# The front of a two-layer graph kernel: statistics, adjacency turns and the first exponentials in another order

## The reference

```
deg = max(sum(adj != 0), 1)
h   = max(layernorm(x), 0)
# layer 0: gated sum of an attention and a plain convolution
attn_a = sigmoid([adj @ h, h] @ Wa.T + ba);   attn_b = sigmoid([adj @ h, h] @ Wb.T + bb)
g  = h @ W_sa;   scores = (g @ a_left)[:, None] + (g @ a_right)[None, :]
e  = where(adj != 0, exp(-leaky_relu(scores, 0.01)), 0)
x_a = (e / (sum(e) + 1e-5)) @ g
x_b = adj @ (h @ W_gcnb) + b_gcnb
x  = x + sigmoid(attn_a * x_a + attn_b * x_b)
# layer 1
h  = max(layernorm(x), 0)
x  = x + relu((dinv * (adj + I) * dinv @ h + h) @ W + b),   dinv = rsqrt(deg)
```

## Time and profile before

| | |
|---|---|
| profiled execution | 611.8 us, its span 610.0 us |
| median of 3 runs | 610.74 us (609.37 to 611.44) |
| TensorE matmuls busy | 593.4 us, 97% of the span, 5265 of them |
| VectorE, ScalarE, GpSimd busy | 425.2, 362.4, 255.5 us |
| mean granted TensorE clock | 0.993 |
| chain that ended last | TensorE 82%, VectorE 5%, DMA 4%, issue 4%, GpSimd 4%, ScalarE 2% |

### The profile page before, as it was taken

The page is one execution under the profiler, slowest core; times in us unless marked ns, Lnnn a source line. Parts: engine busy times, 40 slices in busy tenths (PEclk is TensorE's granted clock), DMA queues, the critical chain, the costliest instruction groups (busy, mean ns, idle before and its releaser), DMA issues.

```text
span 610.0 us, 13250 instructions
## 1 busy us (share of the span) xinstructions
PE 593.4 (97%) x5265; PEld 508.4 (83%) x5265; DVE 425.2 (70%) x811; ACT 362.4 (59%) x878; POOL 255.5 (42%) x361
## 2 busy tenths in 40 slices
PE   7889998999999999999999999999999999999996
PEld 5446687888888888888888888888888888888886
DVE  6897885999998999899989989988753121111111
ACT  3687667797887979797979788979642000000000
POOL 3664313554453435343525276313132374435433
PEclk8999999899999999999999999999999999999999
DMA  8908399957566565647474745010400486546401
GB/s 198 225 3 113 111 134 249 203 83 182 94 150 121 123 134 110 146 98 162 81 177 67 190 52 79 2 19 1 130 2 18 113 318 215 174 157 193 144 20 35
DMA packets 55801, 73.60 MB, mean 121 GB/s; under 512 B 20027, under 2 KB 47933, under 8 KB 54331
## 3 DMA queue, kind: packets, MB, share of 16 engines
q0 software_dynamic: 28544, 22.15, 26.5%
q1 hardware_dynamic: 24754, 46.42, 23.5%
q10 hardware_dynamic: 2441, 4.20, 2.2%
HBM read 69.31 MB, written 22.16 MB: 150 GB/s over the span
## 4 chain that ended last, share of the span: by engine, by line
PE 82%; DVE 5%; DMA 4%; issue 4%; POOL 4%; ACT 2%; ACTq 0%; POOLq 0%; DVEq 0%
PE accE L786 11%; PE accE L788 11%; PE accE L787 11%; PE accA L764 10%; PE accA L765 10%; PE accA L831 7%; PE accA L830 7%; PE accE L830 4%; PE accE L831 4%; DMA stage<-in_adj_dram 3%; POOL stage L369 1%; DVE bst L933 1%; PE pw L803 1%; PE accA L847 1%; PE pw L805 1%
## 5 line engine op out<-in xcount | busy, mean ns | idle before, releaser
L786 PE MATMUL accE<-HI,Z 128*128 128x257 f16 x676 | 185.2, 274 | 2.4 <-DVE wm L1078 2.1
L788 PE MATMUL accE<-HI,E 128*128 128x257 f16 x676 | 184.8, 273 | 0.0
L787 PE MATMUL accE<-LO,Z 128*128 128x256 f16 x676 | 184.7, 273 | 0.0
L549 ACT ACTIVATE Z<-LO,sr 128x256 f32<-128x256 f32 x338 | 151.4, 497 | 35.6 <-PE accE L788 35.6
L764 PE MATMUL accA<-HI,adjT 128*128 128x260 f16 x676 | 154.0, 273 | 0.0
L765 PE MATMUL accA<-LO,adjT 128*128 128x258 f16 x676 | 154.0, 273 | 0.0
L558 ACT ACTIVATE Z<-Z,sr 128x256 f32<-128x256 f32 x338 | 150.1, 496 | 0.2
L1034 DVE TENSOR_TENSOR Z<-adjT,Z 128x512 f32<-128x512 bf16 x169 | 127.0, 751 | 17.1 <-ACT Z L558 16.1
L1040 DVE TENSOR_TENSOR E<-Z 128x512 bf16<-128x512 f32 x169 | 129.0, 763 | 5.8
L369 POOL DMA_DIRECT2D stage<-in_adj_dram x96 | 59.3, 649 | 93.0 <-DVE adjT L1026 88.6
L831 PE MATMUL accA<-LO,adjT 128*128 128x256 f16 x416 | 91.6, 273 | 0.0
(11 more groups left out here) (127 smaller groups left out, 721.0 us busy)
## 6 DMA issues: line engine op xcount, KB each, us to landing
adjT_store<-adjT SPq DMA_DIRECT2D x11, 1664.0 KB, 6.3
stage<-in_adj_dram POOLq DMA_DIRECT2D x48, 192.0 KB, 5.0
stage<-in_adj_dram POOLq DMA_DIRECT2D x36, 224.0 KB, 5.2
adjT<-adjT_store SPq DMA_DIRECT2D x7, 896.0 KB, 6.0
adjT<-adjT_store SPq DMA_DIRECT2D x7, 768.0 KB, 6.0
stage<-adjT_store SPq DMA_DIRECT2D x4, 896.0 KB, 6.4
stage<-adjT_store SPq DMA_DIRECT2D x4, 768.0 KB, 5.8
out_dram<-late ACTq DMA_DIRECT2D x11, 256.0 KB
```

The lines of the kernel that those rows point to most:

```text
L549: ins = act.activation(Z[:, n % RING, v], slw[:, m], ACT.Relu, bias=sr99[:, t:t + 1], scale=1.0 - SLOPE)
L786: pe.matmul(dst[:, 0:D + 1], zhi, HI[:, t, 0:D + 1], start=(t == 0), stop=False)
L787: pe.matmul(dst[:, 0:D], zhi, LO[:, t, 0:D], start=False, stop=False)
L788: ins = pe.matmul(dst[:, 0:D + 1], zlo, HI[:, t, 0:D + 1], start=False, stop=(t == TILES - 1))
```

## The change

- Statistics: one row pair a step (pair s + 4 at step s) instead of two; GpSimd's and VectorE's followers take one pair each instead of batches of one to four. The prologue takes pairs 0 to 5 instead of 0 to 4.
- Adjacency of block 0 is turned in four instructions at steps 4, 5, 6, 7 instead of two and two at 5 and 6; block 1 at 11 to 14 instead of 10 and 11; block 2's first chunk at u = 2 and 4 of block 1, and its second at 7 and 9. `tr_ok` counts each instruction, so all waits on it are doubled.
- Block 0: `neighbours(0, u)` stays at step u + 6, `unit(0, u)` goes to step u + 10 (it was u + 7). `leaky` and `expo` go from u + 5 and u + 6 to u + 8 and u + 9, `mask` and `split` from u + 6 to u + 9. The steps now run to 22; four neighbours of block 1 stand among the last of them.
- TensorE: `turn(1)`, `turn(2)` and `project(0)` stand between the halves of `dense(0)` and `dense(1)`; the first steps are set out anew, with two added waits of ScalarE's `turned` for `project`.
- ScalarE: gate_exp(0), gated_b(0) and el go into block 1 at u = 3, 6 and 1, where they stood before it; gated_b(1) goes into block 2. VectorE: gate_args(0), gates(0), row_sums(0) at u = 1, 3 and 6.
- GpSimd: nbias before the loop over s; loads of block 1 at s = 6 and 8 (were 6 and 7), of block 2 behind the loop.
- SP: the first `spread_left` waits for block 0's adjacency instead of block 1's.

Waits doubled for `tr_ok`, the renamed `first_half(i, e)`, `second_half(i, e)`, `inv_std(i)`, `minus_mean(i)` (one pair or half of what the old ones did), and the removed `batch_of` are left out below.

```diff
+            sp.wait_ge(adj_in[1], adj_count(0, 1))
+            spread_left(0)
             sp.wait_ge(adj_in[1], adj_count(1, 1))
-            spread_left(0)
             keep_adj(0)
             spread_left(1)
...
             load_adj(0, 1)
-            loads = {6: (1, 0), 7: (1, 1), 11: (2, 0), 12: (2, 1)}
+            pool.wait_ge(bias_in, 32)
+            pool.tensor_scalar(nbias[:], bias2[:], -1.0, None, ALU.mult).then_inc(nbias_ok, 1)
+            inv_std(3)
+            inv_std(4)
+            loads = {6: (1, 0), 8: (1, 1)}
             for s in range(PAIRS):
                 score_parts(s)
...
                 gate_columns(s)
+                if s >= 1 and s + 4 < PAIRS:
+                    inv_std(s + 4)
                 if s in loads:
                     load_adj(*loads[s])
+            load_adj(2, 0)
+            load_adj(2, 1)
...
             load_adj(3, 0)
-            pool.wait_ge(bias_in, 32)
-            pool.tensor_scalar(nbias[:], bias2[:], -1.0, None, ALU.mult).then_inc(nbias_ok, 1)
             with_bias(0)
...
             def turned(i):
                 act.wait_ge(hT_ps, i + 1)
+                if 2 <= i <= 3:
+                    act.wait_ge(proj, i - 1)
...
-            for s in range(PAIRS + 7):
+            for s in range(PAIRS + BEHIND + 1):
                 if s == 0:
-                    first_halves(0)
+                    first_half(0, 0)
                 if s + 1 < PAIRS:
                     turned(s + 1)
+                if s == 0:
+                    first_half(0, 1)
                 if s + 2 < PAIRS:
                     norm(s + 2)
-                if 0 <= s - 6 < PAIRS:
-                    expo(0, s - 6)
+                if 0 <= s - BEHIND < PAIRS:
+                    expo(0, s - BEHIND)
...
-            act.wait_ge(srw_ok, PAIRS)
-            act.activation(el[:], srw[:, :, 3], ACT.Exp, scale=SLOPE).then_inc(el_ok, 1)
-            gate_exp(0)
-            gated_b(0)
             for m in range(1, PAIRS):
                 for u in range(PAIRS + 1):
+                    if m == 1 and u == 1:
+                        act.wait_ge(srw_ok, PAIRS)
+                        act.activation(el[:], srw[:, :, 3], ACT.Exp, scale=SLOPE).then_inc(el_ok, 1)
+                    if m == 1 and u == 3:
+                        gate_exp(0)
+                    if m == 1 and u == 6:
+                        gated_b(0)
...
             for s in range(PAIRS):
                 dense(s)
                 if s == 0:
-                    turn(1)
-                    project(0)
+                    keep_busy(5)
+                if s == 1:
                     spread_weights(2, 4, 2)
-                    keep_busy(4)
-                if s == 1:
+                    turn(3)
+                    project(1)
+                if s == 2:
+                    project(2)
                     widen_first()
-                if s + 2 < PAIRS:
+                if 2 <= s and s + 2 < PAIRS:
                     turn(s + 2)
                 if 1 <= s < 4:
                     keep_busy(4)
-                if s >= 6:
-                    neighbours(0, s - 6)
-                if s >= 7:
-                    unit(0, s - 7)
-                if s + 1 < PAIRS:
+                if s >= SUMS_BEHIND:
+                    neighbours(0, s - SUMS_BEHIND)
+                if s > BEHIND:
+                    unit(0, s - BEHIND - 1)
+                if s >= 2 and s + 1 < PAIRS:
                     project(s + 1)
-            for u in range(PAIRS - 6, PAIRS):
-                neighbours(0, u)
-                unit(0, u - 1)
-            unit(0, LAST)
-            for u in range(PAIRS):
+            for s in range(PAIRS, PAIRS + BEHIND + 1):
+                n = s - SUMS_BEHIND
+                neighbours(n // PAIRS, n % PAIRS)
+                unit(0, s - BEHIND - 1)
+            for u in range(BEHIND + 1 - SUMS_BEHIND, PAIRS):
                 neighbours(1, u)
...
+            turns = {4: (0, 0, 0), 5: (0, 0, 1), 6: (0, 1, 0), 7: (0, 1, 1),
+                     11: (1, 0, 0), 12: (1, 0, 1), 13: (1, 1, 0), 14: (1, 1, 1)}
+            for s in range(2, PAIRS + BEHIND):
+                if 2 < s < PAIRS:
                     take_scores(s)
                 if s + 1 < PAIRS:
                     turned_second(s + 1)
+                if s < PAIRS:
+                    second_half(s, 0)
+                    second_half(s, 1)
...
+                if s + 3 < PAIRS:
+                    minus_mean(s + 3)
+                if s + 4 < PAIRS:
+                    row_stats(s + 4)
...
             for m in range(1, PAIRS):
+                after = 2 if m == 1 else 0
                 for u in range(PAIRS):
-                    if u == 4:
+                    if m == 1 and u == 1:
+                        gate_args(0)
+                    if m == 1 and u in (2, 4):
+                        turn_adj(2, 0, (u - 2) // 2)
+                    if m == 1 and u == 3:
+                        gates(0)
+                    if m == 2 and u == 1:
+                        minus_mean1(0)
+                    if u == 4 + after:
                         row_sums(m - 1)
```

More of the change, by code:

```diff
@@ L524, in first_weights, with first_half @@
                 act.activation(dst, src, ACT.Copy, scale=winv[:, (0, 1, 3)[k]:(0, 1, 3)[k] + 1]).then_inc(whi_ok, 1)
-            def first_halves(i):
+            def first_half(i, e):
                 src = dn[:].rearrange("p (e k d) -> p e k d", e=2, k=2)
-                for e in range(2):
-                    act.wait_ge(dn_ps, 2 * i + e + 1)
-                    dst = bass.AP(HI[:].tensor, (2 * i + e) * HIW, [[TILES * HIW, P], [G0, 2], [1, D]])
-                    act.activation(dst, src[:, e], ACT.Copy).then_inc(hi_ok, 1)
+                act.wait_ge(dn_ps, 2 * i + e + 1)
+                dst = bass.AP(HI[:].tensor, (2 * i + e) * HIW, [[TILES * HIW, P], [G0, 2], [1, D]])
+                act.activation(dst, src[:, e], ACT.Copy).then_inc(hi_ok, 1)
             def left_first():
@@ L733, in dense @@
                 for e in range(2):
+                    if i <= 1 and e == 1:
+                        turn(i + 1)
+                    if i == 1 and e == 1:
+                        project(0)
                     if i >= 1:
@@ L938, in row_stats, with minus_mean @@
                 ins.then_inc(stats, 1)
-            def minus_mean(n):
-                a, b = BATCHES[n]
-                dve.wait_ge(rstd_ok, n + 1)
-                dve.scalar_tensor_tensor(out=nmr[:, a:b], in0=mv[:, a:b, :, 0], scalar=-1.0, in1=rstd[:, a:b],
+            def minus_mean(i):
+                dve.wait_ge(rstd_ok, i + 1)
+                dve.scalar_tensor_tensor(out=nmr[:, i], in0=mv[:, i, :, 0], scalar=-1.0, in1=rstd[:, i],
                                          op0=ALU.mult, op1=ALU.mult).then_inc(nmr_ok, 1)
@@ L1129, in _ @@
             row_stats(2)
+            second_half(0, 0)
+            minus_mean(2)
+            turned_second(1)
+            second_half(0, 1)
             dve.wait_ge(w1_in, 16)
@@ L1132, in _ @@
             on_diagonal(2, 4)
-            second_halves(0)
-            minus_mean(2)
+            row_stats(3)
             take_scores(0)
-            turned_second(1)
-            row_stats(3)
-            diagonal_first()
-            scales(2, 4, 2)
-            row_stats(4)
-            minus_mean(3)
-            turns = {5: (0, 0), 6: (0, 1), 10: (1, 0), 11: (1, 1)}
-            for s in range(1, PAIRS + 6):
-                if s < PAIRS:
+            turned_second(2)
+            minus_mean(3)
+            second_half(1, 0)
+            second_half(1, 1)
+            row_stats(4)
+            take_scores(1)
+            scales(2, 4, 2)
+            diagonal_first()
+            minus_mean(4)
+            row_stats(5)
+            turns = {4: (0, 0, 0), 5: (0, 0, 1), 6: (0, 1, 0), 7: (0, 1, 1),
+                     11: (1, 0, 0), 12: (1, 0, 1), 13: (1, 1, 0), 14: (1, 1, 1)}
+            for s in range(2, PAIRS + BEHIND):
+                if 2 < s < PAIRS:
                     take_scores(s)
@@ L1160, in _ @@
                     turn_adj(*turns[s])
-                if 0 <= s - 6 < PAIRS:
-                    mask(0, s - 6)
-                    split(0, s - 6)
-            turn_adj(2, 0)
-            gate_args(0)
-            gates(0)
+                if 0 <= s - BEHIND < PAIRS:
+                    mask(0, s - BEHIND)
+                    split(0, s - BEHIND)
             for m in range(1, PAIRS):
+                after = 2 if m == 1 else 0
                 for u in range(PAIRS):
-                    if u == 4:
+                    if m == 1 and u == 1:
[4 more added lines that the diff above has]
+                        gates(0)
+                    if m == 2 and u == 1:
+                        minus_mean1(0)
+                    if u == 4 + after:
                         row_sums(m - 1)
-                        if m == 1:
-                            turn_adj(2, 1)
-                    if u == 5 and m >= 2:
```

(16 more changed lines are left out.)

97 lines of the change are left out of this document (42 added, 55 removed).

## The result

The change made the kernel slower by 0.9%. The median is 616.35 us (615.23 to 617.81, six runs) against 611.07 us before (609.37 to 611.47, six runs): ratio 1.0094, 95% interval 1.0074 to 1.0114. Forecast were 609.6 us and "same". The profiled execution took 615.71 us (611.8 before), its span 613.9 (610.0), so it shows 3.9 us of the 5.3 between the medians.

A forecast was written before the change was run, and what follows sets the result against it. TensorE's matmuls bound the kernel, with time to win only in the front and the seam at 104.3 us. The first unit at 105.35 instead of 106.52 gains 1.2 us: 610.6 for the profiled execution, median 609.6, range 606.4 to 611.9.

The forecast's parts named there:

- The front to step 9: Front: first four steps give nothing; from step 4 VectorE's shorter steps leave TensorE waits of 1.0, 0.7 and 0.25 us.
- SP's `spread_left(0)` now goes ahead of keep_adj(0) and earlier; nobody waits for it: SP's queue: the earlier store costs nothing, as nobody waits for it before ScalarE's leaky(1, 0) at 87 us.
- 0.5 us of it a short wait of before that the later units don't meet: From dense(12) to the seam: 0.5 of the 1.4 us by which TensorE wants block 1's first unit earlier, at 102.9.
- The seam to block 1: with_bias(0), behind load_adj(3, 0) and quarter (2, 0, 1), holds TensorE 2.45 us plus 1.7 half clock; unit at 105.35.
- rival A: Seam to block 1: clock stays up (607.9 us) or there is no wait at all (605.4 us); chance 0.24.
- At nothing: Block 1's 13 neighbours and what follows: moved turns and gates, 5 us, lie under 28 us of matmuls and cost nothing.
- Rival B: Turn of (2, 0): its load comes late, each microsecond over 19.9 delays the seam; 613.7 us with 24 us; chance 0.08.
- Rival C: Front: early steps are late by their 1.2 us bound and all that follows comes later; 610.8 us; chance 0.10.
- The sum: Whole kernel: 1.2 us gained in all, 611.8 to 610.6 us for the profiled execution, median 609.6.
- The front's gain of 0.85 us: Up to dense(12): it starts at 68.2, against 73.01 less three units, 69.05.

The follow-up runs named there:

- b2: Kernel before the change with only the first spread_left moved to where the change has it, ahead of the wait for block 1's load: 612.17 us, ratio 1.0034.
- a3: Changed kernel with the first spread_left put back behind block 1's load: 612.29 us, ratio 1.0023 to the kernel before.
- a12: Changed kernel without the first store of left scores, its load reading rows of x instead: 613.89 us, ratio 1.0041 to the kernel before.
- a6: Changed kernel with with_bias(0) ahead of load_adj(3, 0) on GpSimd, nothing else: 613.63 us, ratio 1.0043 to the kernel before.
- a1: Changed kernel with both quarters of (2, 1) turned right behind row_sums(0): 611.99 us, ratio 1.0024 to the kernel before.
- a2: Changed kernel with minus_mean1(0) ahead of the turns of (3, 1) on VectorE's queue: 611.72 us, ratio 1.0017 to the kernel before.
- a7: Changed kernel with (2, 1) turned behind row_sums(0), minus_mean1(0) ahead of (3, 1)'s turns, with_bias(0) ahead of load_adj(3, 0): 610.02 us, ratio 0.9993.
- a10: As a7, with the first spread_left made smaller and earlier (blocks 1 to 3) and the second larger (4 to 12): 611.65 us, ratio 1.0013.
- a4: Changed kernel with (2, 1) turned right behind row_sums(0) and the first spread_left back behind block 1's load: 611.97 us, ratio 1.0025.
- a9: Changed kernel with its first spread_left storing 256 elements instead of 1536: 613.25 us, ratio 1.0045 to the kernel before.
- a5: As a4, plus with_bias(0) ahead of load_adj(3, 0) on GpSimd: 614.53 us, ratio 1.0073 to the kernel before.

## Why the prediction was wrong, step by step

- *The front to step 9: right.* Forecast dense(4) at 32.95, dense(9) at 53.7, waits of 1.0, 0.7 and 0.25 us; measured 33.19, 53.78, and 0.99, 0.49, 0.24.
- *"SP's `spread_left(0)` now goes ahead of keep_adj(0) and earlier; nobody waits for it": failed.* True of the semaphores, not of the DMA queues it shares. Forecast dense(10) 57.8, measured 60.21: 2.4 us. The store alone moved (b2), moved back (a3) and left out (a12) all agree.
- *"0.5 us of it a short wait of before that the later units don't meet": failed.* The first unit of block 0 waits 0.7 us for its E at 77.12; before, such a wait was 0.5. From dense(12) to the seam TensorE took 35.7 us instead of 34.7. With dense(12) at 70.77 for 68.2 that puts its arrival at 106.45 for 102.9.
- *The seam to block 1: the mechanism right, with_bias behind the load behind the quarter.* a6 shows it. The wait was 1.56 for 2.45, since TensorE lost more on its way there (3.55 us) than the chain did (2.6). The chain's 2.6 is the store's too: in a3 the unit starts 92.9 us behind dense(0), and the forecast was 105.35 - 12.5 = 92.8; in the kernel after it is 95.4. with_bias took 2.13, between the two prices given. And half of rival A came in: no half clock behind the seam, 1.7 us.
- *"At nothing: ... the turns and gates moved to later u in block 1 (5 us in all) lie under 28 us of matmuls": this is the step that decided.* I counted VectorE's time and not what the moved instructions release. The quarter (2, 1, 1) releases a load, the load's turn stands ahead of `minus_mean1(0)`, and an issue 7.4 us later became 4.2 us of TensorE. a1 and a2, one instruction group each, take it back.
- *Rival B* did not happen in the kernel after (76.06 to 95.77, no wait) but did in a1, a7 and a10, near the margin given: the turn came 20.8, 21.8 and 23.2 us behind the load, after waits of 1.0, 2.0 and 3.4 us, where the forecast had 19.9 us without a wait. *Rival C* was not seen.
- *The sum.* For its own execution the forecast was 610.6 us; 615.7 was measured. The unit at 108.00 for 105.35 is +2.6, the clock kept -1.7, block 2's seam +4.2: together +5.1.
- *The front's gain of 0.85 us: right where no store is in the way.* From dense(0) to dense(12) it was 60.47 us before, less three units 56.51; it is 55.70 in a3 and 55.44 in a12, a gain of 0.8 and 1.1. The late units then take 0.4 back, so that even without the store TensorE came from dense(0) to the seam in 91.4 us (a3) against 91.8: besides these 0.4 us only the seam was to be won.

By medians: undoing block 2's wait gives 4.4 us (a1) or 4.6 (a2), moving the store back 4.1 (a3), leaving it out 2.5 (a12). These do not add up: a4 is a1 and a3 together and no faster than a1. What is given back at one place moves the loads against the turns at the next.

## What to carry to other kernels

When an instruction moves, price what it releases: here a turn 8 us later freed a buffer later, and the load bound a block that the change did not touch; look for the first instruction that stands behind the waiting one on its queue. "Nobody waits for this DMA" holds only for its data: beside a store of single 4-byte elements a load took 11.1 us to land instead of 4.4. Before a redraw, try the single move that its largest term rests on: nbias alone closed the seam of the kernel before, and with_bias ahead of the load closed it in the kernel after.

## What was not expected of the hardware

- A store of 4-byte elements from SBUF to DRAM takes 8.4 us for 256 elements, 11.8 for 1536 with nothing beside it, and 22.7 beside a load. In the kernel after no new packet of any queue went out in 5 of its 12 us. The Trainium skill, "DMA: Bandwidth & Descriptors", Rules for kernel authors, says that a non-contiguous last dimension becomes one descriptor for each element; the trace agrees (some 1550 packets of 4 bytes at 44.0 to 44.9 us).
- A signal from one engine to another can come late by 3 us: [3.07 <-remote] above, with the store under way. This was seen only in kernels with the early store.
- The clock behind an idle gap of TensorE: gaps of 2.22 (before), 2.24 (a4), 2.44 (a9), 2.56 (a6), 2.60 (after), 3.02 (a10), 3.13 (a12) and 4.08 us (a5) were followed by 0.50, the level of 1.2 GHz; gaps of 2.45 (a1), 2.08 (a3) and 1.55 to 1.82 us were not. Each is one execution. The Trainium skill, "TensorE: Matmul & The Clock Gate", "Why this matters for your kernels", names an idle gap from which throughput drops, and only the three longest of these reach it. The trace agrees for those three and differs below: five gaps of 2.2 to 2.6 us were followed by the fall too, and one of 2.45 was not, so a gap of this size is to be priced both ways.
